# Swin window attention and a spiking layer on one core: q's high and low parts spilled and stacked together, and the next sample's normalisation constants computed at other places

## The reference, cut to what matters

```python
# x: (8, 32, 32, 256) f32; windows of 8x8 tokens, 16 heads of 16 channels
def attention(x):                       # _L0
    part = windows(x)                   # (8*16 windows, 64 tokens, 256)
    qkv  = part @ qkv_w.T + qkv_b       # q scaled by 16**-0.5
    attn = softmax(q @ k.T + bias_table[REL_IDX] + MASK)
    return unwindow(attn @ v)
def lif(x):                             # _L1: leaky units over the leading axis of 8 samples
    h = x @ W.T + b
    v = v + (h_t - v) / 2 ; s = (v >= 1) ; v = v * (1 - s)
    return s
def gn(v):                              # group norm, 32 groups of 8 channels, mean and variance over a sample
    return (v - mean) / sqrt(var + 1e-5)
x = x + attention(gn(x))
x = x + lif(gn(x))
```

## Time and profile before

| what | value |
|---|---|
| median of 3 runs | 541.38 us |
| the profiled execution | 540.94 us |
| its span, first to last instruction | 539.2 us |
| PE busy | 81% |
| DVE busy | 75% |
| ACT busy | 70% |
| POOL busy | 52% |
| mean granted TensorE clock | 0.946 of 2.4 GHz |
| DMA | 61.57 MB, 137802 packets, most under 512 B |

### The profile page before, as it was taken

One profiled execution on the slowest core, in us unless ns is written; L12 is line 12 of the kernel. 1 busy time (PEld: TensorE's weight loads), 2 busy tenths in 40 slices (PEclk: granted clock), 3 DMA queues, 4 the chain that ended last, 5 costly groups with the idle time before them and its releaser, 6 DMA issues.

```text
span 539.2 us, 20239 instructions
## 1 busy us (share of the span) xinstructions
PE 435.4 (81%) x7848; PEld 402.3 (75%) x7848; DVE 405.2 (75%) x872; ACT 379.0 (70%) x895; POOL 279.8 (52%) x382
## 2 busy tenths in 40 slices
PE   0346769887888786979887987987798889689997
PEld 0345768887878785978787977987797778578886
DVE  8863658787768675768786889786767787489888
ACT  3372578887878685768886988886787786665551
POOL 5453646666655665356665666755665555740000
PEclk9995889999989898889998999998999998899999
DMA  7144225454554354435554545554435443023333
GB/s 225 48 120 116 72 68 139 116 143 119 128 121 123 107 133 106 120 88 133 128 136 111 132 105 137 134 126 102 100 79 120 117 124 60 2 79 137 136 136 137
DMA packets 137802, 61.57 MB, mean 114 GB/s; under 512 B 108530, under 2 KB 126196, under 8 KB 137716
## 3 DMA queue, kind: packets, MB, share of 16 engines
q1 hardware_dynamic: 137376, 60.33, 42.7%
q10 hardware_dynamic: 340, 0.01, 0.0%
HBM read 35.13 MB, written 25.17 MB: 112 GB/s over the span
## 4 chain that ended last, share of the span: by engine, by line
PE 26%; SPq 20%; issue 15%; POOL 12%; DVE 10%; ACT 9%; DMA 8%; POOLq 1%; ACTq 0%; DVEq 0%
SPq L318 14%; POOL p_lo L457 5%; SPq L312 4%; PE pv_ps L1050 3%; PE proj_ps L928 3%; PE pv_ps L928 3%; PE score_ps L928 3%; DMA q_spill0hi<-q_flat 3%; DMA k_stack<-k_spill0lo 2%; POOL xc L446 2%; PE proj_ps L939 2%; ACT v_hi L531 2%; PE max_ps L928 2%; PE proj_ps L941 2%; PE proj_ps L940 2%
## 5 line engine op out<-in xcount | busy, mean ns | idle before, releaser
L457 POOL TENSOR_TENSOR p_lo<-probs,p_hi 128x512 f16<-128x512 f32 x128 | 148.1, 1178 | 151.4 <-ACT p_hi L614 113.9
L1016 PE MATMUL score_ps<-q_stack,k_stack 96*128 96x64 f16 x1024 | 87.9, 196 | 30.6 <-ACT max_rows L604 11.5
L613 ACT ACTIVATE probs<-score_ps 128x512 f32<-128x512 f32 x128 | 76.9, 601 | 44.2 <-PE score_ps L1026 40.6
L787 DVE TENSOR_REDUCE neg_max<-max_ps 128x16 f16<-128x1024 f32 x64 | 78.4, 1225 | 33.3 <-PE max_ps L996 31.9
L939 PE MATMUL proj_ps<-xn_hi,w_hi 128*128 128x256 f32 x256 | 80.5, 314 | 26.3 <-POOL xn_lo L415 16.2
L1016 PEld LDWEIGHTS score_ps<-q_stack,k_stack 96*128 96x128 f16 x1024 | 73.5, 100 | 37.7 <-ACT max_rows L604 19.0
L1012 PE MATMUL score_ps<-both_parts,bias_k 128*128 128x64 f16 x1024 | 80.1, 196 | 0.0
L781 DVE TENSOR_TENSOR v_lo<-proj_ps,v_hi 64x256 f16<-64x256 f32 x128 | 54.2, 423 | 32.4 <-ACT v_hi L531 30.8
L614 ACT ACTIVATE p_hi<-score_ps 128x512 f16<-128x512 f32 x128 | 77.3, 604 | 0.0
L940 PE MATMUL proj_ps<-xn_lo,w_hi 128*128 128x256 f32 x256 | 75.7, 296 | 0.0
L941 PE MATMUL proj_ps<-xn_hi,w_lo 128*128 128x256 f32 x256 | 75.7, 296 | 0.0
(11 more groups left out here) (130 smaller groups left out, 1193.0 us busy)
## 6 DMA issues: line engine op xcount, KB each, us to landing
xc<-in_x_dram SPq DMA_DIRECT2D x32, 256.0 KB, 3.4
out_dram<-xc SPq DMA_DIRECT2D x32, 256.0 KB, 2.0
q_stack<-q_spill0hi SPq DMA_DIRECT2D x32, 128.0 KB, 2.6
q_stack<-q_spill1hi SPq DMA_DIRECT2D x32, 128.0 KB, 2.7
q_spill0hi<-q_flat SPq DMA_DIRECT2D x16, 128.0 KB, 3.3
k_spill0hi<-k_flat SPq DMA_DIRECT2D x16, 128.0 KB, 3.2
q_spill0lo<-q_flat SPq DMA_DIRECT2D x16, 128.0 KB, 2.7
k_spill0lo<-k_flat SPq DMA_DIRECT2D x16, 128.0 KB, 2.6
```

The source lines that it names most:

```text
L457: pool.tensor_tensor(p_lo[p][:, quads, :, :].rearrange("p g w i -> p (g w i)"), probs[:, quads, :, :].rearrange("p g w i -> p (g w i)"), p ...
L613: act.activation(probs[:, quads, :, :].rearrange("p g w i -> p (g w i)"), score_ps[:, h, :], ACT.Exp)
L787: dve.tensor_reduce(neg_max[:, :].rearrange("p (m n) -> p m n", m=2)[:, :, 0:8], max_ps[:, :, :].rearrange("p m (n j) -> p m n j", j=WS), ...
L1016: pe.matmul(dst, k_stack[slot][0:96, 2 * mid + q, at, :], q_stack[slot][0:96, 2 * mid + q, at, :], start=False, stop=False)
```

## The change

Five edits:

1. q's high and low parts share one DRAM tensor and one spill (256 KB) in place of two (128 KB each), issued once the low parts of q and k are both done. The stack is read in two transfers (64 partitions, then 32) in place of three of 32. k's high part is now the first to be spilled and the first to be read back. `STACKS` goes from 13 to 12 transfers a row.
2. `norm_roots` on POOL, for the samples that have a successor, moves from the end of pair 1 (ahead of the next `xn_lo`) to the start of pair 2 (behind that `xn_lo`, ahead of pair 2's `p_lo`).
3. `norm_moments` of the next sample moves on DVE from pair 0 to the end of pair 7; the row statistics of odd pairs move ahead of `attention_out`.
4. The averages and roots of sample 1 move from ahead of the first pair into pairs 0 to 2 of sample 0, as for every other sample.
5. Ahead of the first pair DVE now does `v_low(1, 2)`, the statistics, `maxima(0)` and the moments in that order.

```diff
@@ q's spills and stacks, SP @@
-        q_spill = [[nc.dram_tensor(f"q_spill{i}{part}", [32, QUADS, HALVES * ROWTOK], f16).ap() for part in ("hi", "lo")] for i in range(2)]
+        q_spill = [nc.dram_tensor(f"q_spill{i}", [2, 32, QUADS, HALVES * ROWTOK], f16).ap() for i in range(2)]
-        STACKS = 13 * 16
+        LO, HI = 0, 1
+        STACKS = 12 * 16
-            def stack_q(slot, first, part):
-                sp.dma_start(q_stack[slot][first:first + 32, :, :, :].rearrange("r g n i -> r (g n i)"),
-                             q_spill[slot][part].rearrange("r g n -> r (g n)")).then_inc(stacked[slot], 16)
+            def spill_q(slot):
+                sp.dma_start(q_spill[slot].rearrange("t r g n -> (r g) t n"), q_flat[:, :, :]).then_inc(q_spilled, 16)
+            def stack_q(slot, rows, kept):
+                sp.dma_start(q_stack[slot][rows, :, :, :].rearrange("r g n i -> r (g n i)"), kept).then_inc(stacked[slot], 16)
             def move_q_and_k(slot, r):
-                sp.wait_ge(q_flat_done, r + 1)
-                spill(q_flat, 0, q_hi_spilled, q_spill[slot][0])
                 sp.wait_ge(k_hi_done, r + 1)
-                spill(k_flat, 0, k_hi_spilled, k_spill[slot][0])
+                spill(k_flat, HI, k_hi_spilled, k_spill[slot][0])
                 sp.wait_ge(k_lo_done, r + 1)
-                spill(q_flat, 1, q_lo_spilled, q_spill[slot][1])
+                spill_q(slot)
                 if not is_first(r, 2):
                     sp.wait_ge(score_ps_done, 4 * (r - 2) + 4)
-                spill(k_flat, 1, k_lo_spilled, k_spill[slot][1])
-                sp.wait_ge(q_hi_spilled, (r + 1) * 16)
-                stack_q(slot, 32, 0)
-                stack_q(slot, 64, 0)
+                spill(k_flat, LO, k_lo_spilled, k_spill[slot][1])
                 sp.wait_ge(k_hi_spilled, (r + 1) * 16)
                 stack_k(slot, 0, 0, slice(0, QUADS))
                 stack_k(slot, 32, 0, slice(0, 2))
                 stack_k(slot, 64, 0, slice(2, QUADS))
-                sp.wait_ge(q_lo_spilled, (r + 1) * 16)
-                stack_q(slot, 0, 1)
+                sp.wait_ge(q_spilled, (r + 1) * 16)
+                stack_q(slot, slice(0, 64), q_spill[slot].rearrange("t r g n -> (t r) (g n)"))
+                stack_q(slot, slice(64, 96), q_spill[slot][HI].rearrange("r g n -> r (g n)"))
                 sp.wait_ge(k_lo_spilled, (r + 1) * 16)
@@ stages of the norm @@
             if has_sample(s, 1):
-                return s + 1, (s + 1) * HALVES, HALVES, -1 if is_first(s, 1) else k
+                return s + 1, (s + 1) * HALVES, HALVES, k
@@ POOL @@
-            norm_roots(pool, root_pool, 0, 1, HALVES, HALVES)
             def pair(n, row, k, s):
                 p = k % 2
+                norm, first, width, stage = norm_beside(s, k)
                 if p == 0 and not is_last_row(row, 2):
                     low_part(k // 2 % 2, row + 3)
+                if stage == 2 and has_sample(s, 1):
+                    norm_roots(pool, root_pool, (norm - 1) * ROOT_STEPS, norm, first, width)
...
-                if stage == 1:
+                if stage == 1 and not has_sample(s, 1):
                     norm_roots(pool, root_pool, (norm - 1) * ROOT_STEPS, norm, first, width)
@@ DVE @@
+            dve.wait_ge(const_step, 11)
+            v_low(1, 2)
             sample_stats(1)
             dve.wait_ge(x_stats_done, 2)
+            maxima(0)
             norm_moments(1, x_stats, 1)
-            dve.wait_ge(const_step, 11)
-            v_low(1, 2)
-            norm_means(1, HALVES, HALVES, spare_averages)
-            norm_spreads(1, HALVES)
-            norm_variances(1, HALVES, spare_averages)
-            maxima(0)
             def pair(n, row, k, s):
-                if k == 0 and has_sample(s, 1) and not is_first(n, 1):
-                    dve.wait_ge(x_stats_done, s + 2)
...
-                if k == 0 and has_sample(s, 1) and not is_first(n, 1):
-                    norm_moments(norm, x_stats, 1)
...
+                if p == 1 and has_sample(s, 2):
+                    dve.wait_ge(x_loaded, row * 16 + (WROWS + 1 if k == BODY - 1 else WROWS + 2) * 16)
+                    measured = row_stats(x_stats, k // 2, row + 2 * WROWS)
+                    if k == BODY - 1:
+                        measured.then_inc(x_stats_done, 1)
+                        dve.wait_ge(x_stats_done, s + 3)
                 if not is_first(n, 1):
                     attention_out(n - 1, (k - 1) % 4, beside)
+                elif beside:
+                    beside()
+                if k == BODY - 1 and has_sample(s, 2):
+                    norm_moments(s + 2, x_stats, 1)
...
-                if p == 1 and has_sample(s, 2):
-                    dve.wait_ge(x_loaded, row * 16 + (WROWS + 1 if k == BODY - 1 else WROWS + 2) * 16)
-                    last = row_stats(x_stats, k // 2, row + 2 * WROWS)
-                    if k == BODY - 1:
-                        last.then_inc(x_stats_done, 1)
@@ PE @@
             project_k(1, 1)
-            average_means(1, HALVES, spare_averages)
             project_v(1, 1)
-            average_variances(1, HALVES, spare_averages)
...
                     weigh_values(n - 1, row if p else row - 1, (k - 1) % BODY, beside)
+                elif beside:
+                    beside()
```

14 lines of the change are left out of this document (6 added, 8 removed).

## The result

The changed kernel took 519.99 us (median of 4 runs, 519.71 to 525.3), beside 541.0 us for the kernel before on the same chip (4 runs, 537.86 to 543.15). The ratio is 0.9639, 95% interval [0.9561, 0.9717]: 3.6% faster. The forecast was 520.5 us, range 509 to 532. The number was right; of its four terms two were too small (the roots and the moments), one was right (ahead of the first pair) and one had the wrong sign (the stacks). That they made up for each other to within 1 us is luck.

The account below looks back on a forecast made before the run. No engine was taken as the bound by itself; PE waited for xn_lo, the moments and the stacks. Gains of 11.5 + 6.4 + 3.7 + 1.1 = 22.7 us, less 2 for the clock, gave 520.5 us, range 509 to 532.

Parts of the forecast that it names:

- Roots behind xn_lo: Pair 3, samples 1 to 6: PE gets xn_lo before asking, max_rows 7.98 us behind pair 2's; gain 11.5 us.
- The 2 us taken off for the clock: Pair 3: PE's new wait for ACT, some 2.1 us, brings half clock in two of six samples; 2 us lost.
- the 524.5 of the rule taken as always true: Pair 3: if a 2.1 us gap always halves PE's clock, the loss is 6 us, the total 524.5.
- Moments in pair 7: First pair of samples 1 to 6: PE's wait for the moments comes back nearly whole; gain 6.4 us.
- The stacks: SP's window rows: two issues fewer, max_rows to operand 11.7 us without a load ahead, 12.9 with; gain 3.7 us.
- Ahead of the first pair: Start and sample 0: maxima(0) 4.85 us earlier, partly paid back in sample 0; 1.1 us left.
- B: Stack path through HBM: becomes the bound at 14.5 us from max_rows to operand; kernel 530 us, chance 0.18.
- D: Stack path: k_lo held behind q's 256 KB transfers, 16.5 us to operand; kernel slower, 553 us, chance 0.05.
- C: SP's issues and PE: stalls and half clock go, all 13.0 us of stack waits return; 509 us, chance 0.12.
- E: Odd pairs: attention_out, held by x's load and row statistics, takes back what was won; 540 us, chance 0.05.

Follow-up runs that it names:

- a1: The changed kernel run once more, unaltered: 523.96 us, ratio 0.9689 to the kernel before.
- x4: The kernel before with only the moments moved to pair 7 and the row statistics ahead of attention_out: 534.08 us, ratio 0.9802.
- x6: The changed kernel with q's two reads last, behind k_lo's four: 538.73 us, ratio 0.9945 to the kernel before.
- x7: The changed kernel with q's two reads first, ahead of k_hi's six: 539.17 us, ratio 0.9962 to the kernel before.
- x11: The changed kernel with q's two reads after two of k_hi's six: 517.98 us, ratio 0.9604 to the kernel before.

## Why the prediction came out right

**Roots behind xn_lo: 11.5 forecast, 14.8 in the trace, 14 alone on the chip.** The mechanism is as it was told: PE's wait gone, ACT's wait for shift in its place, 7.7 us for 7.98. The 3.3 us more are 5 times 0.3 for the shorter way from xn to max_rows, and 1.8 in sample 6, where the pair took only 6.2 us: there PE had waited 1.46 us for the stack in the pair before and then run at half clock, and the roots were done meanwhile.

Part of this gain, and of the moments', may be the clock, as the prediction had it for samples like 3. Over samples 1 to 6 the window view sums (us, then busy us of PE, PEld, DVE, ACT, POOL), before and in the changed kernel:

```profile
sum 315.00, PE 270.14 PEld 252.31 DVE 237.76 ACT 246.10 POOL 187.33; mean PE 45.02 PEld 42.05 DVE 39.63 ACT 41.02 POOL 31.22
```

```profile
sum 300.00, PE 265.17 PEld 248.02 DVE 239.53 ACT 245.64 POOL 187.20; mean PE 44.19 PEld 41.34 DVE 39.92 ACT 40.94 POOL 31.20
```

PE was busy 5 us less with the same matmuls, and DVE, ACT and POOL as long as before. (The second sum takes 2.5 us more than the six samples; cut at the copies of max_rows themselves, PE is busy 270.6 and 263.0 us, 7.6 less.) There was less time at half clock, 10.2 us in these samples for 27.3. How much of the 17.5 us that is worth isn't settled. In a1 the same samples of the same kernel had 20.5 us at half clock and PE was busy 266.3 us, 3.3 more, and yet they took 297.9 us, only 0.4 more.

**The 2 us taken off for the clock: 1.7, by another wait.** This term came out right partly by luck. In pair 3 PE waited five times in samples 1 to 6, for 1.55 to 2.47 us. One of the five, the 2.41 us at 326.39, was followed by half clock, in four windows of 1 us, whose clocks (0.70, 0.50, 0.50, 0.60) are 1.7 us of full work short. It was a wait for the stack and not, as forecast, for ACT. The length doesn't decide it alone: 2.47 and 2.78 us at 277.11 and 301.63 were followed by full clock, and 1.46 at 363.59 by half. In a1 PE waited in pair 3 of all six samples, for 1.35 to 2.56 us; behind three of these waits PE ran at half clock. The wait at 326.39, and the windows behind 277.11, 301.63 and 326.39:

```profile
326.39 0.19 PE L1012 MATMUL score_ps<-q_stack,k_stack 96*128 96x64 f16 x1 [2.41 <-DMA k_stack<-k_spill0lo]
```

```profile
277.00:279.00 2.00, 1.89 (x68) 1.76 (x68) 0.84 (x1) 1.30 (x3) 0.14 (x1) 1.00 0.63 212
301.00:304.00 3.00, 2.37 (x71) 2.24 (x72) 1.32 (x2) 1.78 (x4) 0.62 (x1) 1.00 0.33 112
...
328.00:329.00 1.00, 1.00 (x18) 1.00 (x15) 1.00 (x3) 1.00 (x3) 0.73 (x1) 0.50 0.29 90
```

The Trainium skill (TensorE: Matmul & The Clock Gate, Why this matters for your kernels) warns of idle gaps between bursts of matmuls, after which the engine is back at half rate; its row speaks of longer gaps than these, which the forecast left out. Behind gaps of 1.5 to 2.5 us the clock fell in one of five here, so the trace has it for shorter gaps too, but not as a rule, and the 524.5 of the rule taken as always true didn't come.

**Moments in pair 7: 6.4 forecast, 7.3 in the trace, 10.7 alone [6.5 to 14.9].** The wait came back whole, as told, and the row statistics ahead of attention_out cost nothing: 6 to 7 is unchanged at 37.3, and PE has no wait for attn in samples 1 to 6. The term was 0.9 us too small in the trace, and lies just below the interval of x4.

**The stacks: a gain of 3.7 forecast, nothing or a small loss found. This is the step that failed.** The forecast had the path from max_rows to the operand at 11.7 us without a load ahead and at 12.9 with one, PE's waits at 10 us in all, and the edit worth 3.7. The path is 13.1 us where PE waits, as before, and the waits are 27.3. By its arithmetic the forecast took 12.9, 11.7, 12.9 and 11.7 us for the rows moved in pairs 1, 3, 5 and 7; on average over the six samples they landed at 13.5, 12.4, 13.1 and 13.2. (It puts the first at 19.0 of the sample; 6.35 + 12.9 is 19.25, still in time by its own numbers.) Pair 3's row it took for one without a load ahead, and there is one in five samples of six. Of the path's terms two were too small. The first is the landing: 1.55 taken from the row of before, 2.56 measured, because q's reads are bigger and stand right ahead of the last reads. The second is the start, 2.3 taken for k_hi's spill without a load, where the row above has 2.73. What was right is the reasoning about demand ("the faster engines ask for the stacks sooner"); it was only fed with a path 0.8 us too short on average, and it has the first and the fourth stack of a sample in time, where PE now waits for the first one (in pair 3) in four samples of six, and for the fourth of the sample before (in pair 1) in samples 2, 4 and 6.

In the table this loss sits in pairs that had no wait before, 1 to 2 and 3 to 4, and in the sum it is small: the columns other than 0 to 1 and 2 to 3 went from 210.7 to 215.4, a loss of 4.7 where 3.7 was to be won. These columns hold the clock's 1.7 too, for which 2 were taken off. So they are 4.7 + 3.7 - 2 = 6.4 worse than forecast, and the roots (3.3 more), the moments (0.9), the last sample (2.1) and the head (0.1) are 6.4 better.

**Ahead of the first pair: 1.1 forecast, 1.2 measured**, but as 3.4 won and 2.1 paid back in sample 0, not 4.85 and 3.75.

**The rivals.** B and D, a longer path that becomes the bound, had the right place. The rows of after show paths of 13.8 and 13.9 us in sample 3, and one of 15.2 in sample 4, the longest of all; B wanted 14.5 as a rule and D 15.4. x6 and x7 show that it was near: 0.8 us more and nearly the whole gain is gone, though at 13.9 and not at 15.4. D's price was therefore too mild, if the half clock that came with the longer path counts as a part of it. C, all stack waits gone, is refuted by the 27.3 us. E is refuted by the column 6 to 7.

## What to carry to other kernels

When you take a wait away, ask at once which path is almost as long as the one that you shortened: here a chain of 13 us through HBM had to fit behind two pairs of 11 to 13 us, and it took back a part of every other gain. The price of such a chain isn't in its issues alone; the landing of its last small read depends on the large transfers that were queued just ahead of it, so measure from the last issue to the operand, and keep large reads out of that place (here the landing fell from 2.50 to 2.22 us and the kernel from 524.0 to 516.1, the clock's share in that unknown). And judge each edit of a bundle by itself: one edit of this one was worth nothing, and a right total says little on its terms.

## What was not expected of the hardware

- The position of two reads in a queue of 12, with the same bytes and the same count, moved the kernel from 516.1 us (after four of k_hi's reads) to 538.7 (last) and 539.2 (first).
- A 32 KB read lands in 2.2 us behind 128 KB of q and in 3.1 us behind 384 KB. Four reads of 32 KB put between take it back to 2.2 us (x11).
- The same kernel spent 26.8 us at half clock in one profiled run and 42.5 in another, 520.1 and 524.5 us long. Yet over samples 1 to 6 the two took 297.5 and 297.9 us, with 10.2 and 20.5 us at half clock: so time at half clock isn't by itself time lost.
